# Latent-query attention block: queries of the first token tile alone in the opening, values turned in a bank of their own, ScalarE making the middle part of the keys

## Chip, cores and metric

One NeuronCore of a Trainium2 chip runs the whole program in one launch. The metric is the device time of that launch in microseconds (us). A shorter time is better.

## What is computed

```python
x = x + xattn(layernorm(x), ctx, ctx)      # x (16, 32, 512), ctx (16, 512, 512), 32 heads, 8 kv heads, head 16
x = x + attn(layernorm(x))                 # rotary, causal, 32 tokens, own weights
x = x + x @ w.T + bias                     # w: 512x512 from 3-bit values, one norm per group of 32
...
q = (query @ Wq); k = (key @ Wk); v = (value @ Wv)
scores = jnp.einsum('bhqd,bhkd->bhqk', q, k) * scale
out = jnp.einsum('bhqk,bhkd->bhqd', jax.nn.softmax(scores, axis=-1), v)
...
x_norm = q / 7.0
return (x_norm * (2.0 * n) - n).reshape(-1)
```

The three lines on top are a summary in words; the rest is cut from the reference. All inputs are float32.

## The kernel before

**Engines and order.** The program is written engine by engine (`@block.sync`, `gpsimd`, `scalar`, `vector`, `tensor`); each engine runs its list in order, and semaphores (`wait_ge`, `then_inc`) tie them. Nothing is scheduled by a tool. TensorE is PE in the rows, VectorE is DVE, ScalarE is ACT, GpSimd is POOL, SyncE is SP.

**Tiles.** 512 tokens (16 batches of 32) are four token tiles of 128 rows. The context of a batch is 512 keys by 512 features, loaded already transposed (1 MB). The eight key/value heads are the eight groups g; R = 4 query heads share one.

**Exact products out of bf16.** Keys and queries are split in three bf16 parts: high (a rounded copy), middle (the rounded rest) and low (what is left). For keys: ACT copies bank b_k to `kparts[...,0]` (`key_high`, L576), DVE subtracts to `kres` (`key_residue`, L768), POOL rounds `kres` to the middle part (L468) and subtracts for the low part (L470), both in `key_parts`. Six DMAs of 128 KB from SP (`stack_keys`, L355) copy the parts into six 16-row slots of `kstack`, so that one bf16 matmul adds the six cross products. Queries go through the same four steps (`query_high`, `query_residue`, `query_mid`, `query_low`) into `qparts`, and by six DMAs into `qstack`. The context is split in two f32r parts, `cT_h` (ACT, L611, in the opening L696) and `cT_l` (DVE, L795, in the opening L827), four chunks c each; a projection chunk (`project`, L976 to L978) is three matmuls of 512 columns into b_k or b_v.

**Slots.** After the opening, slot n = 0 to 17 runs a pipeline over batches, with eight steps g: for batch n the scores as rows (L1022, bank b_s or b_x) and their maxima (DVE, L783); for batch n-1 the scores turned, with the maximum taken off by extra rows (L1059, banks b_c), and the exponentials (ACT, L591); for batch n-2 the product with the values (`times_v`, L1001), once per slot behind g = 1. Projection chunks for batches n+1 and n+2 are spread over the steps by the table in `projections`. Values leave b_v through ACT (`vT`, L632, at g = 3), are turned by PE **back into b_v** (L1027, at g = 4), and DVE copies them to `vaug` (`copy_values`, L773, at g = 4); the next V projection (g = 5, chunk 0) writes b_v and waits for that copy (`v_ready`). The middle slots are hardware loops (4 to 11 on PE). In slots 14 and 15 the steps of the second layer are woven in from the table EARLY, the rest follows after slot 17 (LATE).

**SP's order in a slot n:** the context of batch n+3 (waits for the low parts of batch n+1, whose buffer it takes), key parts of batch n+1, query parts of batch n+2.

**The opening.** Context chunks of batch 0, its K and V projection (the last eight matmuls of V begin the fast stretch of PE), layer norm of all four token tiles at once, 16 transposes, then all queries: for each r of four, a sum over four chunks c of f32 matmuls with 512 columns (`first_queries_of`, L1187; each f32 matmul shows as two records), through banks b_c. Then both projections of batch 1, and slot 0. SP sends the first batch's queries as six 32 KB DMAs, then batches 1 to 3 as six of 96 KB (L308). The 3-bit weights are unpacked by DVE between these (`unpack`, L809 to L822) and scaled by POOL in two passes over 128x2048 numbers: times 2n (L555), minus n (L558).

## Time and profile before

| what | value |
|---|---|
| time, median of 3 runs | 336.38 us (335.36 to 337.74) |
| the profiled execution | 338.57 us |
| its span (first to last instruction) | 336.7 us |
| PE busy | 312.5 us, 93% |
| DVE busy | 228.4 us, 68% |
| ACT busy | 186.6 us, 55% |
| POOL busy | 111.0 us, 33% |
| moved by DMA | 41.48 MB, 123 GB/s over the span |

All times in rows are microseconds from the start of the span. A line L768 is line 768 of the kernel before. A busy PE is not PE at its peak: a matmul's record is longer than the distance to the next one, so distances between starts are used.

### The profile page before, as it was taken

The numbers are of one execution on the slowest core, as the hardware profiler recorded it, in microseconds if no ns is written. First come the engines' busy times: TensorE is split into PE (matmuls) and PEld (weight loads), VectorE is DVE, ScalarE is ACT, GpSimd is POOL, SyncE is SP. The second block draws the span as 40 slices with busy tenths as digits, with TensorE's granted clock in tenths as the row PEclk, the third lists the DMA queues.
The fourth block names the chain that finished last, engine by engine and source line by source line (L and its number), as shares of the span: only waits on it lengthen the run. The fifth ranks groups of instructions, "written<-read, shape, count | busy, mean of one in ns | idle before, by whom it ended". The sixth has DMA issues, their size and how long they took to land.

```text
span 336.7 us, 7756 instructions
## 1 busy us (share of the span) xinstructions
PE 312.5 (93%) x2662; PEld 217.2 (64%) x2665; DVE 228.4 (68%) x391; ACT 186.6 (55%) x368; POOL 111.0 (33%) x200
## 2 busy tenths in 40 slices
PE   6699939969999999999999999999999998999996
PEld 2464616647767767767767767766667766766664
DVE  3558778846787777777677687675764369867552
ACT  3344422736876776876776777776766422344220
POOL 1130472422313313313313314224730426662320
PEclk9999967979999999999999999999999999999999
DMA  7991376977769759759879889789500000000002
GB/s 212 412 191 22 135 112 74 202 181 86 180 118 188 180 104 197 185 88 200 184 92 205 182 117 227 181 156 201 146 0 5 2 6 6 9 6 8 2 31 93
DMA packets 39466, 41.48 MB, mean 123 GB/s; under 512 B 19936, under 2 KB 34272, under 8 KB 37216
## 3 DMA queue, kind: packets, MB, share of 16 engines
q1 hardware_dynamic: 39008, 41.00, 59.0%
q8 instruction: 17, 0.28, 0.4%
q10 hardware_dynamic: 432, 0.13, 0.2%
q14 instruction: 9, 0.07, 0.1%
HBM read 24.07 MB, written 1.05 MB: 75 GB/s over the span
## 4 chain that ended last, share of the span: by engine, by line
PE 70%; DVE 12%; DMA 7%; ACT 4%; issue 3%; POOL 2%; SPq 1%; DVEq 0%; ACTq 0%; POOLq 0%
PE b_d L1001 8%; PE b_c L1059 7%; DMA kstack<-kparts 5%; PE b_v L976 4%; PE b_s L1022 4%; PE b_c L1187 4%; PE b_v L977 4%; PE b_v L978 4%; PE b_k L976 3%; PE b_k L978 3%; PE b_k L977 3%; PE b_x L1022 3%; DVE negmax L783 3%; DMA wkv_raw<-in_L_xattn_Wv_dram 2%; DVE vaug L773 2%
## 5 line engine op out<-in xcount | busy, mean ns | idle before, releaser
L591 ACT ACTIVATE region<-b_c 128x512 f32<-128x512 f32 x128 | 74.6, 597 | 46.3 <-PE b_c L1059 26.2
L783 DVE TENSOR_REDUCE negmax<-b_s 128x1 f32<-128x512 f32 x72 | 49.7, 690 | 49.4 <-PE b_s L1022 48.4
L1059 PE MATMUL b_c<-qstack,kstack 108*128 108x128 bf16 x512 | 50.6, 222 | 0.0
L795 DVE TENSOR_TENSOR cT_l<-cx,cT_h 128x512 fp32r<-128x512 f32 x56 | 45.1, 805 | 6.9 <-ACT cT_h L611 6.8
L1059 PEld LDWEIGHTS b_c<-qstack,kstack 108*128 108x128 bf16 x512 | 32.5, 98 | 26.6 <-issue 13.9
L976 PE MATMUL b_k<-cT_h,wkv_h 128*128 128x512 f32 x64 | 36.3, 568 | 7.8 <-DVE cT_l L827 4.2
L477 POOL TENSOR_TENSOR mwide<-negmax,zeros 128x4 bf16<-128x4 f32 x32 | 6.4, 199 | 101.4 <-DVE negmax L783 101.4
L783 DVE TENSOR_REDUCE negmax<-b_x 128x1 f32<-128x512 f32 x56 | 38.2, 681 | 0.9 <-PE b_x L1022 0.8
L976 PE MATMUL b_v<-cT_h,wkv_h 128*128 128x512 f32 x64 | 35.7, 558 | 1.6 <-DVE vaug L773 1.2
L611 ACT ACTIVATE cT_h<-cx 128x512 fp32r<-128x512 f32 x56 | 35.0, 628 | 0.0
L1022 PE MATMUL b_s<-kstack,qstack 96*128 96x512 bf16 x72 | 28.1, 391 | 6.4 <-DMA kstack<-kparts 3.3
L1001 PE MATMUL b_d<-region,vaug 128*17 128x128 f32 x1024 | 31.5, 275 | 0.0
L468 POOL TENSOR_TENSOR kparts<-kres,zeros 128x512 bf16<-128x512 f32 x16 | 18.6, 1161 | 37.8 <-DVE kres L768 37.8
L1001 PEld LDWEIGHTS b_d<-region,vaug 128*17 128x17 f32 x1024 | 26.8, 98 | 2.0 <-issue 0.4
L978 PE MATMUL b_k<-cT_l,wkv_h 128*128 128x512 f32 x64 | 26.7, 418 | 0.2 <-issue 0.2
L977 PE MATMUL b_k<-cT_h,wkv_l 128*128 128x512 f32 x64 | 26.5, 415 | 0.0
L977 PE MATMUL b_v<-cT_h,wkv_l 128*128 128x512 f32 x64 | 26.1, 408 | 0.0
L583 ACT ACTIVATE qstack<-b_d 12x512 bf16<-12x512 bf16 x32 | 18.9, 589 | 13.1 <-PE b_d L988 12.3
L978 PE MATMUL b_v<-cT_l,wkv_h 128*128 128x512 f32 x64 | 26.0, 407 | 0.0
L1022 PE MATMUL b_x<-kstack,qstack 96*128 96x512 bf16 x56 | 22.2, 396 | 0.0
L976 PEld LDWEIGHTS b_k<-cT_h,wkv_h 128*128 128x128 f32 x64 | 13.1, 205 | 10.7 <-DVE cT_l L795 3.8
L470 POOL TENSOR_TENSOR kparts<-kres,kparts 128x512 bf16<-128x512 f32 x16 | 18.9, 1181 | 1.3
(357 smaller groups left out, 584.7 us busy)
## 6 DMA issues: line engine op xcount, KB each, us to landing
cx<-in_ctx_dram SPq DMA_DIRECT2D x15, 1024.0 KB, 5.9
kstack<-kparts SPq DMA_DIRECT2D x96, 128.0 KB, 5.3
qstack<-region SPq DMA_DIRECT2D x76, 32.0 KB, 3.3
cx<-in_ctx_dram SPq DMA_DIRECT2D x4, 256.0 KB, 4.8
xs<-in_x_dram SPq DMA_DIRECT2D x1, 1024.0 KB, 9.4
region<-in_L_xattn_Wq_dram SPq DMA_DIRECT2D x1, 1024.0 KB, 11.6
cx<-in_L_xattn_Wo_dram SPq DMA_DIRECT2D x1, 1024.0 KB, 10.1
cx<-in_L_attn_Wq_dram SPq DMA_DIRECT2D x1, 1024.0 KB, 7.0
```

The costliest lines, as they stand in the source:

```text
L470: nc.gpsimd.tensor_tensor(kparts[:, m % 2, 2], kres[:], kparts[:, m % 2, 1], ALU.subtract).then_inc(k_low, 1)
L583: nc.scalar.activation(qstack[STACK:ROWS, HALF * half:HALF * half + HALF, m % 4], m_rows[STACK:ROWS].unsqueeze(1).to_broadcast([MROWS, HAL ...
L591: nc.scalar.activation(pT[:, g], b_c[g % 2][:].rearrange("p (a n) -> p a n", a=KT), ACT.Exp, scale=SCALE).then_inc(exp_ready, 1)
L611: nc.scalar.activation(cT_h[:, c], cx[:, m % 2, c], ACT.Copy).then_inc(ctx_high, 1)
L783: nc.vector.tensor_reduce(negmax[:, n % 2, g:g + 1], score_bank(n, g, trip)[:], AX, ALU.max, negate=True).then_inc(max_ready, 1)
L795: nc.vector.tensor_tensor(cT_l[:, c], cx[:, m % 2, c], cT_h[:, c].bitcast(F32), ALU.subtract).then_inc(ctx_low, 1)
L976: nc.tensor.matmul(out, wkv_h[:, which, c], cT_h[:, c], start=(c == 0), stop=False)
L977: nc.tensor.matmul(out, wkv_l[:, which, c], cT_h[:, c], start=False, stop=False)
L978: last = nc.tensor.matmul(out, wkv_h[:, which, c], cT_l[:, c], start=False, stop=(c == C - 1))
L1001: last = nc.tensor.matmul(b_d[TILE * j:TILE * j + VW, P * half:P * half + P], vaug[:, m % 4, a, g], pT[:, g, a], start=(a == 0), stop=(a = ...
L1022: nc.tensor.matmul(score_bank(n, g, trip)[:], qstack[0:STACK, g, n % 4], kstack[0:STACK, n % 4, g], start=True, stop=True).then_inc(s_read ...
L1059: last = nc.tensor.matmul(b_c[g % 2][:, P * a:P * a + P], kstack[0:ROWS, m % 4, g, P * a:P * a + P], qstack[0:ROWS, g, m % 4], start=True, ...
```

## The change

1. **Queries by token tile.** `first_queries_of(t, rows)` makes the queries of one token tile t: 16 matmuls of 128 columns each. Tile 0 (batches 0 to 3) is made in the opening; tiles 1 to 3 are made in halves in slot 0, one half in each of the steps g = 0 to 5. Their splits stand on ACT and DVE in slot 0 too. The tokens are loaded as one 256 KB piece (tile 0) and one of 768 KB, with `xwq` between them. The statistics and the row turns are done for tile 0 first. The query DMAs of the opening are six of 128 KB for batches 0 to 3 together.
2. **Unpacking** by DVE moves into slot 0 (g = 0 to 5) and gives 2q/7 - 1, so that POOL scales in one pass, cut in four, in slot 1.
3. **Values** are turned into b_t (up to slot 13) at g = 5, and copied by DVE at g = 6. A V projection waits only until ACT has emptied b_v.
4. **ACT makes the middle part of the keys** (`key_mid`), at g = 3 of the slot, ahead of `vT`. POOL makes only the low part.
5. Moved besides in the opening: `zeros` set first and 11 warming passes for 9, ACT takes all four context chunks ahead of the V weights, key parts of batch 1 move into slot 0 (as do its last projection chunks), the context of batch 2 is loaded behind the key parts of batch 0.

```diff
-                sp.dma_start(xs[:], xf).then_inc(x_loaded, 16)
+                sp.dma_start(xs[:, 0], xf[:, 0]).then_inc(x_loaded, 16)
                 sp.dma_start(xwq, xwq_d.rearrange("(c p) r n -> p c r n", p=P)).then_inc(xwq_loaded, 16)
+                sp.dma_start(xs[:, 1:TILES], xf[:, 1:TILES]).then_inc(xs_loaded, 16)
                 load_ctx(1, 0)
-                sp.wait_ge(ctx_low, C)
-                load_ctx(2, 0)
...
                     stack_keys(0, part)
-
+                sp.wait_ge(ctx_low, C)
+                load_ctx(2, 0)
+                for part, done in ((0, q_high), (2, q_low)):
+                    sp.wait_ge(done, 1)
+                    first_queries_part(sp, part)
                 sp.wait_ge(ctx_low, 2 * C)
                 load_ctx(3, 0)
...
             def key_parts(m, trip):
-                wait(pool, k_res, 1, m, 1, trip)
                 wait_ring(pool, kstack_loaded, m - 2, trip, SLOTS)
-                nc.gpsimd.tensor_tensor(kparts[:, m % 2, 1], kres[:], zeros[:], ALU.add).then_inc(k_mid, 1)
                 wait(pool, k_mid, 1, m, 1, trip)
...
+            def scale_weights(t):
+                some = slice(NGRP // TILES * t, NGRP // TILES * (t + 1))
+                nc.gpsimd.tensor_tensor(wide[:, some], wide[:, some], wnorm[:, some].unsqueeze(2).to_broadcast([P, NGRP // TILES, GS]),
+                                        ALU.mult).then_inc(w_ready, 1)
...
+            def key_mid(m, trip):
+                wait(act, k_res, 1, m, 1, trip)
+                wait_ring(act, kstack_loaded, m - 2, trip, SLOTS)
+                nc.scalar.activation(kparts[:, m % 2, 1], kres[:], ACT.Copy).then_inc(k_mid, 1)
...
+                    if splits_keys(n, g - 2, trip):
+                        key_mid(n + 1, trip)
                     if g == 3 and live(n + 1, trip):
...
+                    if not looped(trip) and n == 0 and g in (2, 4, 6):
+                        query_residue(g // 2)
+                    if not looped(trip) and n == 0 and g in (3, 5, 7):
+                        query_low(g // 2)
+                    if not looped(trip) and n == 0 and g < 6:
+                        unpack(g)
...
-                    if g == 4 and live(n + 1, trip):
-                        copy_values(n + 1, trip)
+                    if g == 6 and live(n + 1, trip):
+                        copy_values(n + 1, value_bank(n, trip), trip)
...
-                    wait(pe, v_ready if which else k_res, 1, m, 0, trip)
+                    wait(pe, vT_ready if which else k_res, 1, m, 0, trip)
...
+            def first_queries_of(t, rows):
+                pe.wait_ge(xhT_ready, t + 1)
+                count(pe, q_res, t - 1)
+                for r in rows:
+                    for c in range(C):
+                        last = nc.tensor.matmul(b_c[t % 2][:, P * r:P * r + P], xwq[:, c, r], xhT[:, c, P * t:P * t + P],
+                                                start=(c == 0), stop=(c == C - 1))
+                if rows.stop == R:
+                    last.then_inc(q_summed, 1)
...
-                    if g == 4 and live(n + 1, trip):
-                        wait(pe, vT_ready, 1, n + 1, 1, trip)
-                        for a in range(KT):
-                            last = nc.tensor.transpose(b_v[:, P * a:P * a + P], vT[:, P * a:P * a + P], ident[:])
-                        last.then_inc(v_transposed, 1)
+                    if g == 5 and live(n + 1, trip):
+                        turn_values(n + 1, value_bank(n, trip), trip)
...
+                    if not looped(trip) and n == 0 and g < 6:
+                        first_queries_of(1 + g // 2, range(R // 2 * (g % 2), R // 2 * (g % 2 + 1)))
```

PE in the opening, before: the rows after the V projection of batch 0. `region` as an input is `xh` under L1204 and `xwq` with `xhT` under L1187.

```order
L1180 MATMUL b_c<-zeros 128x512 x4
L1204 MATMUL b_x<-ident_sb,region 128x128 [waits xh_ready,ident_loaded]
L1204 MATMUL b_s<-ident_sb,region 128x128 [waits xh_ready]
L1204 MATMUL b_c<-ident_sb,region 128x128 [waits xh_ready]
L1208 MATMUL b_v<-ident_sb,vT 128x128 [waits vT_ready]
L1187 MATMUL b_c<-region 128x512 [waits xwq_loaded,xhT_ready]
```

The same place after the change (L1229 turns rows, L1049 makes queries, L1035 turns values).

```order
L1229 MATMUL b_c<-ident_sb,region 128x128 [waits xh_ready,ident_loaded]
L1221 MATMUL b_c<-zeros 128x512 x3
L1049 MATMUL b_c<-region 128x128 [waits xhT_ready,xwq_loaded]
L1049 MATMUL b_c<-region 128x128 x15
L1229 MATMUL b_x<-ident_sb,region 128x128 [waits xh_ready]
L1229 MATMUL b_s<-ident_sb,region 128x128 [waits xh_ready]
L1035 MATMUL b_t<-ident_sb,vT 128x128 [waits vT_ready]
L1001 MATMUL b_k<-cT_h,wkv_h 128x512 [waits k_res,ctx_low]
```

Sixteen matmuls of 512 columns became sixteen of 128 in this place; the other 48 of 128 stand in slot 0, as in this piece of PE's list (its steps g = 2 and g = 5).

```order
L1064 MATMUL b_s<-kstack,qstack 128x512 [waits max_ready]
L1001 MATMUL b_k<-cT_h,wkv_h 128x512 [waits k_res,ctx_low]
L1049 MATMUL b_c<-region 128x128 [waits q_res,xhT_ready]
L1049 MATMUL b_c<-region 128x128 x7
...
L1064 MATMUL b_x<-kstack,qstack 128x512 [waits max_ready]
L1035 MATMUL b_t<-ident_sb,vT 128x128 [waits v_ready,vT_ready]
L1001 MATMUL b_v<-cT_h,wkv_h 128x512 [waits vT_ready,ctx_low]
```

In step g = 5 the turn now stands ahead of the V projection and goes to b_t; in the list before it stands one step earlier and goes to b_v.

ACT in a slot of the loop, before.

```order
L583 ACTIVATE qstack<-b_d 12x4x128 [waits pv_ready]
L626 ACTIVATE o_raw<-b_d 128x256 [waits oraw_transposed,pv_ready]
L591 ACTIVATE region<-b_c 128x512 [waits pv_ready,st_ready]
L276 REGISTER_ALU [waits v_chunk]
L632 ACTIVATE vT<-b_v 128x512 [waits v_transposed]
```

And after.

```order
L597 ACTIVATE qstack<-b_d 12x4x128 [waits pv_ready]
L640 ACTIVATE o_raw<-b_d 128x256 [waits oraw_transposed,pv_ready]
L605 ACTIVATE region<-b_c 128x512 [waits pv_ready,st_ready]
L590 ACTIVATE kparts<-kres 128x512 [waits kstack_loaded1,k_res]
L277 REGISTER_ALU [waits v_chunk]
L648 ACTIVATE vT<-b_v 128x512 [waits v_transposed]
```

The middle part of the keys (L590) stands behind the third exponential of the slot and ahead of the copy of the values.

## Rows read from the trace of the kernel before

**Rows 1.** Windows by stage: length, busy and count by engine, PEclk, DMA share, GB/s.

```profile
23.00:36.50 13.50, 13.48 (x33) 6.07 (x33) 10.85 (x24) 5.71 (x10) 1.35 (x2) 1.00 0.37 108
44.00:57.20 13.20, 9.32 (x29) 5.26 (x30) 11.13 (x13) 0.87 (x3) 5.27 (x6) 0.61 0.82 100
57.20:71.30 14.10, 10.48 (x71) 6.92 (x70) 9.85 (x15) 9.42 (x17) 5.52 (x14) 1.00 0.97 185
...
85.60:227.30 141.70, 139.31 (x1511) 100.70 (x1509) 106.03 (x177) 102.77 (x200) 43.28 (x112) 1.00 0.85 165
```

**Rows 2.** Timeline, opening and slot 0: start, duration, engine, line, operation, idle before.

```profile
11.04 1.27 POOL L547 TENSOR_TENSOR wkv_l<-wkv_raw,wkv_h 128x512 fp32r<-128x512 f32 x1 [9.26 <-ACT wkv_h L712]
...
15.64 0.63 PE L976 MATMUL b_v<-cT_h,wkv_h 128*128 128x512 f32 x1
...
19.39 1.04 PE L1180 MATMUL b_c<-zeros 128*128 128x512 bf16 x4
...
23.02 14.00 PE L1187 MATMUL b_c<-region 128*128 128x512 f32 x32 [0.41 <-ACT region L727]
...
44.02 0.38 PE L1022 MATMUL b_s<-kstack,qstack 96*128 96x512 bf16 x1 [1.52 <-DMA qstack<-region]
...
44.83 3.64 POOL L558 TENSOR_TENSOR region<-region,wnorm 128x2048 f32<-128x2048 f32 x1
45.04 3.98 DVE L795 TENSOR_TENSOR cT_l<-cx,cT_h 128x512 fp32r<-128x512 f32 x1
...
49.08 0.79 PE L976 MATMUL b_k<-cT_h,wkv_h 128*128 128x512 f32 x1 [3.29 <-DVE cT_l L795]
```

**Rows 3.** Timeline, slot 1 and the start of slot 2.

```profile
57.04 0.36 SPq L349 DMA_DIRECT2D cx<-in_ctx_dram  x1
...
71.31 0.39 PE L1022 MATMUL b_s<-kstack,qstack 96*128 96x512 bf16 x1 [3.10 <-DMA kstack<-kparts]
```

**Rows 4.** The page's DMA issues: count, KB each, us from issue to landing.

```profile
xs<-in_x_dram SPq DMA_DIRECT2D x1, 1024.0 KB, 9.4
```

**Rows 5.** Windows, one stretch of the opening; the last two numbers are DMA share and GB/s.

```profile
24.00:26.00 2.00, 2.00 (x6) 0.93 (x5) 1.28 (x4) 0.00 (x0) 1.35 (x2) 1.00 0.45 87
```

**Rows 6.** Timeline of PE, one slot of the loop (136.81 to 149.65).

```profile
136.81 0.38 PE L1022 MATMUL b_s<-kstack,qstack 96*128 96x512 bf16 x1
...
137.27 0.40 PE L977 MATMUL b_k<-cT_h,wkv_l 128*128 128x512 f32 x1
...
143.68 0.38 PE L1022 MATMUL b_s<-kstack,qstack 96*128 96x512 bf16 x1
144.09 0.66 PE L1027 MATMUL b_v<-ident_sb,vT 128*128 128x128 f32 x4
...
145.53 0.38 PE L1022 MATMUL b_x<-kstack,qstack 96*128 96x512 bf16 x1
...
146.37 0.40 PE L977 MATMUL b_v<-cT_h,wkv_l 128*128 128x512 f32 x1
...
149.65 0.38 PE L1022 MATMUL b_s<-kstack,qstack 96*128 96x512 bf16 x1
```

**Rows 7.** Timeline of POOL and ACT in the next slot (from 149.65).

```profile
152.97 1.16 POOL L468 TENSOR_TENSOR kparts<-kres,zeros 128x512 bf16<-128x512 f32 x1 [1.88 <-DVE kres L768]
...
155.36 0.60 ACT L591 ACTIVATE region<-b_c 128x512 f32<-128x512 f32 x1
```

**Rows 8.** Key DMAs (L355): the last two of that slot, then all 96.

```profile
L355 SPq DMA_DIRECT2D kstack<-kparts x2: 594/597/600, 154.8 to 155.4; - x2
DMA to landing us min/median/max: 6.1/6.4/6.6
...
DMA to landing us min/median/max: 3.3/5.3/8.3
```

**Rows 9.** Weight loads of L1187 (group, mean ns); f32 matmuls of 128 columns in the tail.

```profile
L1187 PEld LDWEIGHTS b_c<-region 128*128 128x128 f32 x32 | 6.0, 190 | 7.8 <-issue 7.2 <-ACT region L727 0.6
...
296.56 1.09 PE L1155 MATMUL b_k<-kstack,vaug 128*64 128x128 f32 x16
```

More of the change, by code:

```diff
@@ L289, in splits_keys @@
         def splits_keys(n, g, trip):
-            return g == 1 and (looped(trip) or 1 <= n < B - 1)
+            return g == 1 and (looped(trip) or n < B - 1)
         def wait_queries(eng, m, trip):
@@ L381, in opening @@
                     stack_keys(0, part)
+                sp.wait_ge(ctx_low, C)
[3 more added lines that the diff above has]
+                    first_queries_part(sp, part)
                 sp.wait_ge(ctx_low, 2 * C)
                 load_ctx(3, 0)
-                for part, done in ((0, q_high), (2, q_low)):
-                    sp.wait_ge(done, R)
-                    first_queries_part(sp, part, 0, 1, first_queries)
-                for part in range(3):
-                    first_queries_part(sp, part, 1, 4, next_queries)
             def slot(n, trip):
@@ L414, in slot @@
                         stack_keys(m, part)
+                if not looped(trip) and n == 1:
+                    sp.wait_ge(q_low, TILES)
                 if live(n + 2, trip) and (looped(trip) or n >= 2):
@@ L505, in slot @@
                     max_parts(n, 0, trip)
+                if not looped(trip) and n == 1:
+                    pool.wait_ge(unpacked, 1)
+                    for t in range(TILES):
+                        scale_weights(t)
                 if n == B - 2:
@@ L1003, in times_v, with turn_values @@
                 last.then_inc(pv_ready, 1)
+            def turn_values(m, bank, trip):
+                wait(pe, vT_ready, 1, m, 1, trip)
+                wait(pe, v_ready, 1, m, 0, trip)
+                for a in range(KT):
+                    last = nc.tensor.transpose(bank[:, P * a:P * a + P], vT[:, P * a:P * a + P], ident[:])
+                last.then_inc(v_transposed, 1)
             def projections(n, g, trip):
-                if not looped(trip) and (n, g) in ((0, 0), (0, 1), (0, 3)):
-                    return []
                 ahead, which, c = ((1, 0, 3), (1, 1, 2), (2, 0, 0), (1, 1, 3), (2, 0, 1), (2, 1, 0), (2, 0, 2), (2, 1, 1))[g]
                 return [(n + ahead, which, c)] if live(n + ahead, trip) else []
+            def first_queries_of(t, rows):
+                pe.wait_ge(xhT_ready, t + 1)
+                count(pe, q_res, t - 1)
+                for r in rows:
+                    for c in range(C):
+                        last = nc.tensor.matmul(b_c[t % 2][:, P * r:P * r + P], xwq[:, c, r], xhT[:, c, P * t:P * t + P],
+                                                start=(c == 0), stop=(c == C - 1))
+                if rows.stop == R:
+                    last.then_inc(q_summed, 1)
             def slot(n, trip):
@@ L1198, in opening @@
                     project(0, 1, c, 0)
-                warm(4)
                 pe.wait_ge(ident_loaded, 16)
-                for t in range(TILES):
-                    pe.wait_ge(xh_ready, t + 1)
-                    for c in range(C):
-                        last = nc.tensor.transpose((b_x, b_s, *b_c)[t][:, P * c:P * c + P], xh[:, t, P * c:P * c + P], ident[:])
-                    last.then_inc(xh_transposed, 1)
-                pe.wait_ge(vT_ready, 1)
-                for a in range(KT):
-                    last = nc.tensor.transpose(b_v[:, P * a:P * a + P], vT[:, P * a:P * a + P], ident[:])
-                last.then_inc(v_transposed, 1)
-                for r in range(R):
-                    first_queries_of(r)
-                for which in range(2):
-                    for c in range(C):
-                        project(1, which, c, 0)
+                turn_rows(0)
+                warm(3)
+                pe.wait_ge(xwq_loaded, 16)
+                first_queries_of(0, range(R))
+                turn_rows(1)
+                turn_rows(2)
+                turn_rows(3)
+                turn_values(0, b_t, 0)
+                for which, c in ((0, 0), (0, 1), (0, 2), (1, 0), (1, 1)):
+                    project(1, which, c, 0)
+                pe.wait_ge(xhT_ready, TILES)
             opening()
```

186 lines of the change are left out of this document (90 added, 96 removed).

## The prediction

> **What bounds the kernel now.** I read the windows by stage first, to see where PE, the busiest engine, is not full; then the timeline across each hole; then one slot of the loop, start by start; last the DMAs, since they feed both holes.
>
> The windows [rows 1] show five stages. From 23 to 36.5 PE is full with the first queries. Slot 0 (44.0 to 57.2) has PE at 9.32 of 13.20 us and a granted clock of 0.61. Slot 1 (57.2 to 71.3) has PE at 10.48 of 14.10. Slots 3 to 13 (85.6 to 227.3) are eleven slots of 141.70/11 = 12.88 us with PE at 98%: here PE is the bound, unless its records hide waits. What comes after slot 13 isn't touched by the change.
>
> The timeline [rows 2] says what makes the early holes. The queries of all four tiles take PE from 23.02 for 14.00 us, and slot 0 can't start before their parts have gone through ACT, DVE and a DMA: 44.02, ended by `qstack`. At 45.04 a DVE subtraction of 512 columns lasts 3.98 us, as long as POOL's second scaling pass beside it (44.83, 3.64 us for four times the columns); PE waits 3.29 us for it. A granted clock of 0.61 over the slot says that most of it ran at the lower of the two levels, 1.2 GHz, and this is the slot in which PE stood still. Slot 2 starts at 71.31 after 3.10 us of waiting for `kstack` [rows 3].
>
> In the loop [rows 6], a score and the first pass behind it take 137.27 - 136.81 = 0.46 us when nothing waits. At g = 5 the same pair takes 146.37 - 145.53 = 0.84: 0.38 us of wait for DVE's copy of the values out of b_v. At g = 4 the turn of the values starts 0.41 behind the score instead of 0.23: 0.18 us of wait for ACT's `vT`. So each slot of 149.65 - 136.81 = 12.84 us holds some 0.56 us of waits inside what looks full.
>
> **Opening, up to slot 0.** V's weights bound its projection from below: POOL has their low part at 11.04 + 1.27 = 12.31, but PE began V at 15.64, behind K [rows 2]. ACT now takes the context chunks first, so K is done by about 12.3 and V starts there. V took 19.39 - 15.64 = 3.75 us; at the spacing of 0.23 of the loop [rows 6] it takes 2.8, to 15.1, and with all of it slow 17. The tokens of tile 0 come early enough: all of them land 3.55 + 9.4 = 12.95 [rows 4], 768 KB less at some 400 GB/s is 11.0; statistics, two small activations and 0.5 us of normalising end near 13. Turning tile 0 takes 0.45 (four transposes), ACT's copy 0.6, so its queries start near 16.3. How long they take the trace doesn't show: no f32 matmul has 128 weight columns and 128 moving ones. L1187 shows 14.00/32 = 0.4375 us per record of 512 columns [rows 2], a quarter is 0.11. From below this is the end. From above, the weight load of L1187 (0.19 us [rows 9]) would set the pace if it hid behind nothing. The nearest row is L1155, 64 weight columns against 128: 1.09/16 = 0.068 per record, below its own weight load, so loads do hide. I take 0.12: 32 records, 3.8 us, to 20.1.
>
> The Trainium skill, "TensorE: Matmul & The Clock Gate", sections "LDWEIGHTS (loading the stationary operand)" and "Weight-path perf modes", speaks against this edit: a weight load costs its columns divided by 1.2 in ns whatever the moving side, and the fast load is not for FP32, so cutting 512 columns into 4 times 128 makes four times the loads. L1187's 190 ns per load is no shorter than that rule's 107 ns; L1155 shows such loads hidden. By the rule unhidden this is a rival, below.
>
> Behind the first queries come three tile turns (1.3 us), the value turn (0.45), and nine matmuls of batch 1's projections. Six of those wait: the third context chunk is on ACT behind two row copies, the middle part and two DMA issues, ready near 26.5. PE would arrive at slot 0 at about 28.6 to 30, and its idle of 3 us there may cost clock.
>
> But the DMA comes later. Before, key parts of batch 0, context 2 and the small loads were through at about 25, where the busy share drops to 0.45 [rows 5]. The same bytes stand ahead of the queries now. The six query DMAs are 128 KB each, like a key DMA, and two of those land 160.9 and 162.0, 1.05 apart [rows 8]. 25 + 6 x 1.05 = **31.3** for the start of slot 0, for 44.02. Bounds: 28.6 if the DMAs keep up, 35 if ACT's two DMAs and the small packets add their own time.
>
> **Slots 0 and 1.** PE's work in slot 0: 8 scores x 0.23 = 1.8; 8 projection chunks x 0.70 = 5.6; 48 f32 matmuls, 96 records x 0.12 = 11.5; turns 0.7. Sum 19.6. DVE: before, 11.13 less the 3.3 of stall = 7.8; from the stretch 23 to 36.5, 10.85 less four context subtractions (2.65) = 8.2; some 1.9 more for the rest of the unpacking, one query pair less, a key residue. Sum 17.9, just under PE, and its last context subtraction falls at about 20.5. That one releases SP's load of context 4, and here the end is set by the same chain as before: load issued 57.04, keys landed and slot 2 begun 71.31, 14.3 us [rows 3]. It is a queue of 1 MB, the constants and six key DMAs, and POOL's low part comes only about 1 us later in slot 1, so it hides in that queue. Slot 2 starts at 31.3 + 20.5 + 14.3 = 66.1, for 71.31: **-5.2 us**. So two thirds of the 12.7 us won in the opening go back, because slot 0 now carries 48 matmuls. Bounds: -8 with 28.6, and +3.8 with records of 0.19 (128 x 0.07 = 9 more).
>
> POOL's one pass of 4 x 0.9 us stands in slot 1, behind both key and maximum parts. It can still stretch a DVE subtraction by 0.9; PE waits for keys at the end of that slot in any case, so nothing. If that cover went it would cost up to 1 us. The 3.65 us pass that is dropped and the stall of 3.29 are inside the account of slots 0 and 1.
>
> **Slots 2 to 13, twelve of them.** The two value waits go (up to 0.56 each). What is late next? ACT gains 0.63 us per slot, at 72% before (102.77/141.70 [rows 1]); its exponential behind the new copy is needed a step later, so that hides. The keys don't. POOL began the middle part at 152.97, that is 3.3 us into the slot; ACT can only begin behind the exponential of 155.36 to 155.96, 6.3 into it [rows 7]. Middle part ready at 6.9, low part at 8.1: 2.5 us later than before. SP's last key DMA goes at about 8.25 into the slot. Behind it in SP's list stand the six query DMAs and the next context load, all 2.5 us later too; neither is needed within the slot. Before, the last key DMA was issued 5.75 in and landed 155.4 + 6.6 = 162.0, 12.35 in, just ahead of the next start at 162.5: the queue was full, so a later issue costs less than it is late. With the least landing of 3.3 us for the first middle DMA (issue 6.95, lands 10.3) and 1.05 for each of the two behind, the keys land at 12.4. The slot can't be shorter than about 12.5, while PE alone would allow 12.3. Gain 0.35 per slot, 12 x 0.35 = **-4.2 us**. Bounds: -6.7 (12 x 0.56), and above zero if landings stay at today's.
>
> **Sum.** The profiled execution is 338.57 us (2.2 above the median shown). 338.57 - 5.2 - 4.2 = 329.2; the same 9.4 off the median 336.38 gives **327.0**.
>
> **Rivals.**
> A, the loop wins nothing: with 4.6 us of landing for the low part (8.25 + 4.6 = 12.85) the key wait takes exactly the place of the value waits. For: DMA share 0.85 over the loop. Against: the landings of 6.1 to 6.6 contain the queue. 336.38 - 5.2 = 331.2.
> B, weight loads set the pace: 0.19 per record, slot 2 starts 3.8 later than before; 336.38 + 3.8 - 4.2 = 336.0, no change. For: the 190 ns load. Against: L1155.
> C, slower: the late middle part. If the low part's DMA still takes the row's 6.1 us [rows 8] from its issue at 8.25, it lands at 14.35, and every slot ends there: 12 x 1.5 = 18 - 5.2 = +12.8, 349.2. It decides from a landing of 5.35 on (slot of 13.6, where 12 x 0.75 outweighs 5.2 by 1%); the median of all is 5.3, which speaks for it, but those DMAs stood behind three high parts and 1 MB, and now the queue would have run nearly empty.
> D, the opening wins nothing: slot 0 grows by as much as it starts earlier, because DVE and PE wait for each other on its chain of query splits. Then only the loop: 332.2.
>
> The Trainium skill, "DMA: Bandwidth & Descriptors", section "Issuing engines are not separate DMA queues", says that DMAs from several engines run on the same 16 engines. By that, the two middle query DMAs on ACT's queue win nothing over SP's, as the sum has it; no row here shows the two queues apart.
>
> **How the numbers follow.** Forecast 0.55 (its own range 322 to 331.5), A 0.15, B 0.10, C 0.07, D 0.08, and 0.05 for both gains near their upper bounds (about 321). Low 319.5 takes in the last; high 334 takes in A and D and leaves out B and C, 0.17. A difference of 1% (3.4 us) is about what a measurement of this kernel can tell from no change: faster than 333.0 holds the forecast, most of A and over half of D, 0.77; within 1% most of B and the rests, 0.16; slower C, 0.07.
>
> **What would show it.** Right: the first score at about 31, its wait ended by `qstack`; slot 2 at about 66 after a wait for `kstack`; 32 records of queries in about 3.8 us; slots of 12.5 us in the loop, no wait for `vaug` or `vT` before b_v's matmuls, and small waits for `kstack` at slot starts. Wrong: queries at 6 us (B); slots of 12.85 (A) or over 13.5 (C) with scores waiting for `kstack` each time; slot 0 of more than 25 us with PE waiting for DVE (D).

## The result and the profile after

The changed kernel takes 346.29 us (median of 4 runs, 344.89 to 349.12), the kernel before in the same session 337.06 us (335.36 to 338.42): ratio 1.029, 95% interval 1.020 to 1.037. It is slower by 9 us, where 9.4 us less were forecast. Medians here are over all runs of a kernel, ratios only over those that didn't fall into a slower state of the chip, so the two can differ by about 1%. The profiled execution took 349.12 us with a span of 347.3, 10.6 more than the 336.7 of before. I call slot n the time from the first score of batch n to the first score of batch n+1; the starts come from the timeline of PE.

| | before | after | predicted |
|---|---|---|---|
| slot 0 starts | 44.02 | 35.22 | 31.3 |
| slot 0, slot 1 long | 13.18, 14.11 | 20.94, 15.48 | 20.5, 14.3 |
| slot 2 starts | 71.31 | 71.64 | 66.1 |
| slots 2 to 13 | 155.96 | 164.11 | 151.8 |
| slot 14 long | 14.57 | 16.66 | as before |
| from there to the end | 94.86 | 94.89 | as before |

So 0.3 + 8.15 + 2.1 = 10.6 us, and nearly all of it lies in the loop. Windows by stage, with the columns of [rows 1]: the end of the opening, slot 0, slot 1, slots 3 to 13. Each line has the window and its length, the busy us of PE, of its weight loads, of DVE, ACT and POOL, then the granted clock, the DMA share and GB/s.

```profile
23.00:35.20 12.20, 4.43 (x22) 3.11 (x21) 2.90 (x5) 3.46 (x7) 0.34 (x1) 0.93 1.02 233
35.20:56.20 21.00, 20.98 (x134) 18.93 (x134) 15.66 (x30) 6.43 (x12) 2.36 (x5) 0.88 0.22 41
56.20:71.60 15.40, 10.65 (x71) 6.91 (x70) 11.38 (x18) 10.84 (x20) 9.23 (x17) 0.98 0.86 162
86.90:235.70 148.80, 138.79 (x1507) 103.50 (x1507) 101.39 (x177) 107.48 (x210) 36.29 (x100) 0.98 0.73 158
```

PE did the same work in the loop (138.79 us busy against 139.31) in 148.80 us instead of 141.70. It stood still for 2.4 us of it before and does for 10 us now. The DMA share fell from 0.85 to 0.73, so the queues weren't fuller either. What PE waits for stands in the page's groups; the number behind the bar is busy time, the last part idle time and what ended it.

```profile
L475 POOL TENSOR_TENSOR kparts<-kres,kparts 128x512 bf16<-128x512 f32 x16 | 18.6, 1163 | 121.3 <-ACT kparts L590 121.3
...
L1064 PE MATMUL b_s<-kstack,qstack 96*128 96x512 bf16 x72 | 28.3, 393 | 20.7 <-DMA kstack<-kparts 12.7
```

The same scores before:

```profile
L1022 PE MATMUL b_s<-kstack,qstack 96*128 96x512 bf16 x72 | 28.1, 391 | 6.4 <-DMA kstack<-kparts 3.3
```

The first scores of the slots now wait 12.7 us in all for `kstack`, for 3.3 before, and POOL's low part waits 121.3 us for ACT's middle part. The timeline has the single waits (PE; its idle time is in brackets): after slot 1 as in [rows 3], then at the end of slot 4 and of slot 12.

```profile
35.22 0.58 PE L1064 MATMUL b_s<-kstack,qstack 96*128 96x512 bf16 x1 [4.99 <-DMA qstack<-region]
71.64 0.61 PE L1064 MATMUL b_s<-kstack,qstack 96*128 96x512 bf16 x1 [3.26 <-DMA kstack<-kparts]
113.84 0.39 PE L1064 MATMUL b_s<-kstack,qstack 96*128 96x512 bf16 x1 [2.16 <-DMA kstack<-kparts]
221.53 0.61 PE L1064 MATMUL b_s<-kstack,qstack 96*128 96x512 bf16 x1 [4.81 <-DMA kstack<-kparts]
```

The slots don't share the loss evenly. Slots 8 to 11 take 12.44, 12.38, 12.41 and 12.38 us with no such wait, 0.4 us less than the 12.84 of before. Slots 4 to 7 take 14.67, 14.11, 13.75 and 13.14, and slots 12 and 13 take 17.08 and 14.22. The waits aren't the whole price: three stretches behind waits, in slots 2, 5 and 13, ran at a granted clock of 0.54 to 0.59.

```profile
71.60:78.40 6.80, 6.76 (x71) 4.82 (x74) 2.58 (x4) 1.42 (x3) 0.00 (x0) 0.54 0.52 147
116.00:119.40 3.40, 3.40 (x63) 2.53 (x65) 0.84 (x2) 0.48 (x2) 0.00 (x0) 0.59 1.04 267
221.50:225.20 3.70, 3.67 (x15) 2.51 (x16) 2.16 (x4) 1.11 (x2) 0.00 (x0) 0.58 0.92 304
```

PE is counted busy there, only slower. (The expectations below name slots 4 to 7 also by the starts they end with, 5 to 8.)

The chain of waits across slot 4 names what carries the delay: POOL's low part, its DMA, PE.

```profile
101.16 4.89 issue
106.05 0.03 POOLq L277
106.08 0.00 issue
106.08 1.17 POOL kparts L475
107.26 0.02 issue
107.27 6.45 DMA kstack<-kparts
113.72 0.12 issue
113.84 0.39 PE b_s L1064
```

And SP's list in slot 4 (99.17 to 113.84), where L367 sends queries, L356 loads a context and L362 sends key parts:

```profile
96.27 4.08 SPq L367 DMA_DIRECT2D qstack<-region  x6
100.63 0.36 SPq L356 DMA_DIRECT2D cx<-in_ctx_dram  x1
101.04 6.83 SPq L362 DMA_DIRECT2D kstack<-kparts  x6
108.10 3.93 SPq L367 DMA_DIRECT2D qstack<-region  x6
112.29 1.34 SPq L356 DMA_DIRECT2D cx<-in_ctx_dram  x1
```

The query DMAs run until 100.35, past the start of the slot, because they stand behind late key parts. So the 1 MB context load goes out 1.46 us into the slot, 0.4 ahead of the high key parts. It took 10.2 us to land (5.7 in the slot before). The low part, issued 8.1 us into the slot as worked out, then took 6.45 us to land. In the settled slot from 167.28 the last three key DMAs took 3.5 to 4.2. There too the queries run past the start of the next slot (180.10 for 179.66) and the context load goes out 0.65 us into it, but 1.2 us ahead of the key parts. So an overrun alone doesn't yet make a slot long.

### The profile page after: what moved, and what is told of

Read it like the earlier page. It is cut to its first block, busy times and chain, and to the rows that moved or that the text cites. A ratio compares the mean times of both kernels' runs of the same rounds, so it can differ in the third digit from the quotient of the medians.

```text
span 347.3 us, 7973 instructions
## 1 busy us (share of the span) xinstructions
PE 312.2 (90%) x2759; PEld 229.0 (66%) x2762; DVE 218.5 (63%) x391; ACT 194.5 (56%) x386; POOL 97.0 (28%) x185
## 3 DMA queue, kind: packets, MB, share of 16 engines
HBM read 24.07 MB, written 1.05 MB: 72 GB/s over the span
## 4 chain that ended last, share of the span: by engine, by line
PE 39%; issue 28%; DMA 11%; POOL 8%; DVE 8%; ACT 3%; SPq 2%; POOLq 0%; ACTq 0%; DVEq 0%
PE b_c L1049 4%; PE b_d L1026 3%; DMA kstack<-kparts 3%; DMA qstack<-region 3%; PE b_c L1100 3%; DMA cx<-in_L_attn_Wq_dram 2%; PE b_s L1064 2%; DMA wkv_raw<-in_L_xattn_Wv_dram 2%; DVE negmax L804 2%; POOL mwide L486 2%; POOL kparts L475 1%; PE b_v L1001 1%; PE b_v L1003 1%; PE b_v L1002 1%; PE b_v L1126 1%
## 5 line engine op out<-in xcount | busy, mean ns | idle before, releaser
L475 POOL TENSOR_TENSOR kparts<-kres,kparts 128x512 bf16<-128x512 f32 x16 | 18.6, 1163 | 121.3 <-ACT kparts L590 121.3
L1064 PE MATMUL b_s<-kstack,qstack 96*128 96x512 bf16 x72 | 28.3, 393 | 20.7 <-DMA kstack<-kparts 12.7
L822 DVE TENSOR_TENSOR cT_l<-cx,cT_h 128x512 fp32r<-128x512 f32 x56 | 38.8, 693 | 0.6 <-ACT cT_h L625 0.6
L1001 PE MATMUL b_v<-cT_h,wkv_h 128*128 128x512 f32 x64 | 36.4, 569 | 0.5 <-POOL wkv_l L562 0.5
L1026 PE MATMUL b_d<-region,vaug 128*17 128x128 f32 x1024 | 32.7, 282 | 0.0
L1026 PEld LDWEIGHTS b_d<-region,vaug 128*17 128x17 f32 x1024 | 27.5, 101 | 2.6 <-issue 0.6
L1064 PEld LDWEIGHTS b_s<-kstack,qstack 96*128 96x128 bf16 x72 | 7.0, 97 | 30.3 <-issue 14.7
L1003 PE MATMUL b_k<-cT_l,wkv_h 128*128 128x512 f32 x64 | 25.8, 404 | 0.0
L584 ACT ACTIVATE kparts<-b_k 128x512 bf16<-128x512 f32 x16 | 9.5, 596 | 20.1 <-PE b_k L1003 19.8
```

The lines of the kernel that those rows point to most:

```text
L475: nc.gpsimd.tensor_tensor(kparts[:, m % 2, 2], kres[:], kparts[:, m % 2, 1], ALU.subtract).then_inc(k_low, 1)
L822: nc.vector.tensor_tensor(cT_l[:, c], cx[:, m % 2, c], cT_h[:, c].bitcast(F32), ALU.subtract).then_inc(ctx_low, 1)
L1001: nc.tensor.matmul(out, wkv_h[:, which, c], cT_h[:, c], start=(c == 0), stop=False)
L1003: last = nc.tensor.matmul(out, wkv_h[:, which, c], cT_l[:, c], start=False, stop=(c == C - 1))
L1026: last = nc.tensor.matmul(b_d[TILE * j:TILE * j + VW, P * half:P * half + P], vaug[:, m % 4, a, g], pT[:, g, a], start=(a == 0), stop=(a = ...
L1064: nc.tensor.matmul(score_bank(n, g, trip)[:], qstack[0:STACK, g, n % 4], kstack[0:STACK, n % 4, g], start=True, stop=True).then_inc(s_read ...
```

## Experiments

Theory T says that the late middle part on ACT is the cause; the rivals are named in each expectation. The first four ran together.

**e1**, part 4 undone in the slots.

```diff
+                if looped(trip) or m > 0:
+                    wait(pool, k_res, 1, m, 1, trip)
+                    nc.gpsimd.tensor_tensor(kparts[:, m % 2, 1], kres[:], zeros[:], ALU.add).then_inc(k_mid, 1)
                 wait(pool, k_mid, 1, m, 1, trip)
...
-                    if splits_keys(n, g - 2, trip):
-                        key_mid(n + 1, trip)
```

> The changed kernel with the middle part of the keys made by POOL again in the slots (part 4 undone there, all else kept). Theory T, the copy on ACT stands too late (6.3 us into the slot, POOL's began 3.3 us into it) and holds up SP's list: the 12.7 us of waits for kstack at slot starts between 71 and 230 us and the 2 us of slot 15 go, slots of 12.3 to 12.45, time about 332 to 334. Rival R1, the value turn one step later and its copy by DVE at g = 6 make the context parts and so SP's loads late: waits stay, 344 to 347. Rival R2, the loads of the opening, pushed back, put the transfers of all later slots out of step: waits stay too, 343 to 347, and slots 5 to 8 are the long ones again.

Measured: 330.19 us, ratio 0.983 (0.977 to 0.989). Part 4 alone costs 16 us. The time is below the range of T. Of the waits for `kstack` in the loop two are left, ahead of slots 5 and 13 (1.62 and 1.56 us). Slots 2, 3 and 5 to 11 take 12.08 to 12.71 us, most of them 12.20. Slot 4 is long here too (14.04), but the next one is at 12.17 again: such a disturbance can arise without the late part, and doesn't last then. What starts it I haven't found. R1 and R2 fall.

From the start of slot 2 to that of slot 14, e1 takes 150.80 us and the change 164.11. About 6 of these 13.3 us are longer waits ahead of slots (9.4 for 3.5 in sum). About 6 more lie behind waits: slot 2 takes 15.27 for 12.08, slot 13 takes 14.22 for 12.79, and slot 5, nearly without a wait of its own, 14.11 for 12.17. Those are the three stretches at the lower clock shown above, which e1 hasn't got (its granted clock is 1.00 from 68.30 to 75.10, and behind its waits of 1.62 and 1.56 us as well).

**e2**, the same copy on ACT, one step earlier.

```diff
-                    if splits_keys(n, g - 2, trip):
-                        key_mid(n + 1, trip)
...
+                    if splits_keys(n, g - 1, trip):
+                        key_mid(n + 1, trip)
                     if g == 2 and live(n - 1, trip):
                         exponentials(n - 1, 0, trip)
```

> The changed kernel with ACT's middle part one step earlier, at g = 2 ahead of the first two exponentials, where ACT idles 1.3 us per slot. T: begins about 3.1 us into the slot, the low part is there at 4.9 for 8.1, waits for kstack go; time 331 to 333, slots of 12.3 to 12.45. If the exponentials, 0.6 us later, hold up PE: slots of 12.6 to 13, 335 to 339. R1 and R2: waits for kstack stay, 344 to 347.

Measured: 328.60 us, ratio 0.980 (0.973 to 0.987). This again is below the range of T. Slots 5 to 11 take 12.20 each without a wait. The engine wasn't wrong, the place was: ACT idled just ahead of the exponentials. In its slot from 92.01 (ACT, POOL and SP), the middle part starts 3.3 us into the slot for 6.2, and SP is through with the queries at 101.98, 2.3 us before the next context load at 104.30:

```profile
92.13 0.34 SPq L356 DMA_DIRECT2D cx<-in_ctx_dram  x1
93.88 3.95 SPq L362 DMA_DIRECT2D kstack<-kparts  x6
95.32 0.63 ACT L590 ACTIVATE kparts<-kres 128x512 bf16<-128x512 f32 x1 [0.95 <-DVE kres L789]
96.03 1.16 POOL L475 TENSOR_TENSOR kparts<-kres,kparts 128x512 bf16<-128x512 f32 x1 [1.88 <-ACT kparts L590]
98.05 3.93 SPq L367 DMA_DIRECT2D qstack<-region  x6
104.30 0.34 SPq L356 DMA_DIRECT2D cx<-in_ctx_dram  x1
```

**e3**, part 4 alone on the kernel before (the `key_mid` of the diff at g = 3, POOL's copy left out for batches from 2 on).

> The kernel before with this alone: ACT makes the middle part of the keys at g = 3 in the slots (the opening as it was, values turned in b_v at g = 4). T: waits for kstack come up at slot starts, 343 to 349. R1 and R2: no change, 336 to 338.

Measured: 341.17 us, ratio 1.017 (1.010 to 1.024), between the ranges, nearer to T's; waits for `kstack` do come up (0.84 ahead of slot 7, 2.74 ahead of slot 13), as T said. The same edit costs 4.4 us on slots of 12.84 and 16 us on slots of 12.2. My reading is that it got dear by what part 3 had won; this isn't shown, for the kernel in which it costs 16 has the new opening too, and parts 3 and 4 were not run together on the old one.

**e4**, part 3 alone on the kernel before.

```diff
-                    wait(pe, v_ready if which else k_res, 1, m, 0, trip)
+                    wait(pe, vT_ready if which else k_res, 1, m, 0, trip)
...
-                    if g == 4 and live(n + 1, trip):
+                    if g == 5 and live(n + 1, trip):
                         wait(pe, vT_ready, 1, n + 1, 1, trip)
...
-                            last = nc.tensor.transpose(b_v[:, P * a:P * a + P], vT[:, P * a:P * a + P], ident[:])
+                            last = nc.tensor.transpose(bank[:, P * a:P * a + P], vT[:, P * a:P * a + P], ident[:])
```

> The kernel before with part 3 alone: values turned in b_t at g = 5, copied by DVE at g = 6. By the rows of the loop the two value waits (0.38 and 0.18 us) go: slots of 12.3 if keys allow it, 12 x 0.56 = 6.7 less, 330 to 331; with keys landing 12.35 into the slot as before, slots of 12.4 to 12.7 and 332 to 335. R1: waits for kstack come up, 340 or more.

Measured: 331.61 us, ratio 0.987 (0.983 to 0.990). Slots of 12.20, 0.64 less than before where 0.56 was worked out. e1 is e4 with the new opening: 330.19 against 331.61. The opening and slot 0 together win 1.4 us, less than the scatter of either.

**e5** asks why lateness adds up over slots. A constant `SENT = 3` takes the place of `SLOTS` in `stack_queries` and in the waits for `qstack_loaded`; all else is the changed kernel.

```diff
-                for s in range(SLOTS):
+                for s in range(SENT):
                     sp.dma_start(qstack[HD * s:HD * s + HD, :, m % 4],
```

> The changed kernel with three of the six query DMAs of a slot left out (batches 4 to 15; the three rows they would fill keep older numbers, so part of the scores is not computed from its own queries). The late middle part on ACT stays. Theory S, the late key parts hurt because SP's list (context load 0.6, keys to about 8.7 us, queries 3.9 us behind them) is then as long as a slot of 12.2 to 12.4, so that one late slot pushes the next context load into the next key parts (its landing was 10.2 us at 100.63, for 5.7 at 87.61): SP is 2 us shorter, the chain of late slots ends at once, at most one slot over 13, time 334 to 338. Rival L, it is the keys' own lateness (low part ready 8.1 us into the slot and 4 to 6.5 us of landing behind it) and no list: slots 5 to 8 stay at 13.1 to 14.7 each and the time at 343 to 347.

Measured: 336.09 us (333.67 to 341.24), ratio 0.995 (0.991 to 0.999). The time is in the range of S. Slots 4 to 11 take 12.32 to 12.59, the chain of late slots is gone; slots 2, 12 and 13 stay over 13, where S allowed one. ACT and POOL are as late as ever; only SP's list has room (its slot from 98.43):

```profile
98.16 0.34 SPq L357 DMA_DIRECT2D cx<-in_ctx_dram  x1
100.17 6.94 SPq L363 DMA_DIRECT2D kstack<-kparts  x6
104.62 0.62 ACT L591 ACTIVATE kparts<-kres 128x512 bf16<-128x512 f32 x1
105.32 1.17 POOL L476 TENSOR_TENSOR kparts<-kres,kparts 128x512 bf16<-128x512 f32 x1 [5.64 <-ACT kparts L591]
107.34 2.00 SPq L368 DMA_DIRECT2D qstack<-region  x3
110.63 0.34 SPq L357 DMA_DIRECT2D cx<-in_ctx_dram  x1
```

The middle part starts 6.2 us into the slot here too, but SP is free at 109.34 and the next load goes out at 110.63, ahead of the slot's start (110.87). Three DMAs of 32 KB less are also less traffic; e11 leaves the traffic as it is.

**e11** leaves nothing out and turns SP's order about in the changed kernel.

```diff
                     load_ctx(n + 3, trip)
+                if live(n + 1, trip) and (looped(trip) or n >= 3):
+                    sp.wait_ge(st_ready, passed)
+                    stack_queries(n + 1, trip)
...
-                if live(n + 2, trip) and (looped(trip) or n >= 2):
-                    sp.wait_ge(st_ready, passed)
-                    stack_queries(n + 2, trip)
```

> The changed kernel, nothing left out, with SP's order turned about: the six query DMAs of a batch go one slot later, directly behind the context load instead of ahead of it (and so ahead of the key parts, not behind them). ACT still makes the middle part at g = 3. The bytes and the number of issues are those of the changed kernel. Theory S, the late key parts hurt by pushing the query DMAs and with them the next context load behind the start of the slot: the load goes out within 0.3 us of every slot's start, slots 4 to 7 come to 12.2 to 12.8, 334 to 339 us. Rival N, e5 gained by its three missing DMAs, that is by their packets in the queues: slots 4 to 7 stay at 13 and more, 343 to 347.

Measured: 339.60 us (335.30 to 341.27), ratio 1.002 (0.998 to 1.006): the median lies just above the range of S, the ratio within it. The sign that S named is there only in part. The context load goes out with the start of the slot (112.21 for 112.20) or ahead of it (124.41 for 125.56, where a slot ends in a wait), but slots 3, 4, 5, 7 and 9 still take 14.19, 13.74, 13.36, 13.94 and 13.32, where S had 12.2 to 12.8 for 4 to 7.

**e12** puts the same order on e8 (below), whose middle part is early.

> The kernel of e8 with the same order of SP's list. There the middle part comes early and the list has 2 us to spare, so S expects next to nothing in slots 4 to 11; the query DMAs now compete with the key parts for the queues just before these are waited for: 323 to 327, 2 us more at most.

Measured: 332.35 us (326.72 to 334.88), ratio 0.973 (0.963 to 0.983), against 324.28 and 0.960 for e8. The expectation missed: the order itself costs 4 us by the ratios and 8 by the medians, and six of the slots from 3 to 13 now start with a wait for keys, for one in e8, since the keys stand behind the queries. The same is likely for the long slots of e11. With this order e11 and e12 are 7 us apart by the medians and 10 by the ratios, opening included; with the order of the change the late middle part costs 16. That fits SP's list carrying a part of the loss, but doesn't size it: in the turned order a late part can also hide behind waits that are there without it, and the pairs differ in the opening and in the stretches at the lower clock. A run with the change's order, its bytes and a shorter list on SP (some of the queries issued by another engine) would have parted the two; there is none.

**e6** turns to the opening, which won 8.8 us at slot 0 and nothing at slot 2. On e2, SP's query DMAs go ahead of the load of context 2.

```diff
-                sp.wait_ge(ctx_low, C)
-                load_ctx(2, 0)
                 for part, done in ((0, q_high), (2, q_low)):
                     sp.wait_ge(done, 1)
                     first_queries_part(sp, part)
+                sp.wait_ge(ctx_low, C)
+                load_ctx(2, 0)
```

> The kernel of e2 with one thing turned about in the opening: the four query DMAs of SP go ahead of the 1 MB load of context 2. Theory D, slot 0 waits for query parts that stand behind 1 MB in busy DMA queues (busy share 1.0 to 1.1 from 20 to 32 us; the query DMAs took 5.6 to 8.9 us to land): slot 0 starts at 30.9 to 31.3 (PE is done at 30.8) for 33.17, and slot 2 starts about 2 us earlier, 65.5 to 66.5 for 67.82; time 326 to 327 for 328.6. Rival P, slot 0 has to wait for the context instead, or slot 2's start hangs on something else: slot 0 earlier, slot 2 as before, 328 to 329.

Measured: 328.15 us (323.68 to 329.93). Slot 0 starts at 30.63 for 33.17, with no wait, and slot 2 at 64.24 for 67.82, more than D asked for. The time doesn't follow and lies in the range of P. The profiled spans are 325.0 and 325.4: slots 2 and 3 take 13.70 and 12.81 for 12.09 and 12.10, and slots 7 and 12 another 0.8 and 0.9 more. The windows behind the start of slot 2, first of e2, then of e6, show the reason in the third column from the right, the granted clock.

```profile
67.80:70.00 2.20, 2.18 (x14) 1.49 (x15) 1.66 (x3) 0.98 (x2) 0.00 (x0) 1.00 0.97 410
```

```profile
64.20:66.50 2.30, 2.26 (x10) 1.58 (x11) 1.29 (x2) 0.72 (x2) 0.00 (x0) 0.63 0.70 292
66.50:70.20 3.70, 3.70 (x74) 2.69 (x73) 1.29 (x2) 1.80 (x4) 1.16 (x1) 0.77 0.45 113
```

PE had waited 2.03 us there in e2 and 2.55 in e6, and in e6 it ran partly at 1.2 GHz afterwards.

**e7** fills PE's idle time in the opening with the queries of tile 1.

```diff
-                for which, c in ((0, 0), (0, 1), (0, 2), (1, 0), (1, 1)):
+                for which, c in ((0, 0), (0, 1)):
                     project(1, which, c, 0)
+                first_queries_of(1, range(R))
                 pe.wait_ge(xhT_ready, TILES)
+                for which, c in ((0, 2), (1, 0), (1, 1)):
+                    project(1, which, c, 0)
...
-                    if not looped(trip) and n == 0 and g < 6:
+                    if not looped(trip) and n == 0 and 2 <= g < 6:
```

Tile 3 is turned through bank b_v for this, as b_c is taken.

> e6, and besides the 16 matmuls of token tile 1 (32 records, 3.8 us) taken out of slot 0 and put into the opening where PE stands idle for 3.4 us for the context (23.8 to 27.2). Theory F, slots 0 and 1 are bound by PE's 11.5 us of f32 matmuls put there: slot 0 starts at 31 to 32 and is 16.3 to 17 us long for 20.16, slot 2 starts at 62 to 63.5, time 322.5 to 324.5. Rival V, DVE (14.85 us busy in slot 0) or SP's chain of loads bounds slots 0 and 1: slot 0 over 18.5 us or slot 1 longer by as much, 326 to 328.

Measured: 327.98 us (322.74 to 330.45), ratio 0.977 (0.968 to 0.986). Slot 0 starts at 28.73 and slot 2 at 64.28, as in e6: the 3.8 us taken out of slot 0 came back. The timeline and the windows of PE show how.

```profile
34.07 0.77 PE L1001 MATMUL b_k<-cT_h,wkv_h 128*128 128x512 f32 x1 [3.09 <-DVE kres L789]
34.63 0.63 PE L1002 MATMUL b_k<-cT_h,wkv_l 128*128 128x512 f32 x1
35.06 0.63 PE L1003 MATMUL b_k<-cT_l,wkv_h 128*128 128x512 f32 x1
35.49 3.62 PE L1049 MATMUL b_c<-region 128*128 128x128 f32 x16
```

```profile
28.70:34.07 5.37, 2.25 (x9) 1.31 (x10) 4.16 (x11) 1.74 (x4) 0.00 (x0) 0.93 0.70 275
34.07:38.00 3.93, 3.93 (x15) 3.65 (x16) 2.23 (x5) 1.00 (x2) 1.16 (x1) 0.50 1.05 132
```

By its lengths and its median this is rival V, though slot 0 starts earlier than expected and the profiled run, 322.74 us, is the quickest of the four. With steps 0 and 1 empty PE runs into the key chain, and after the wait of 3.09 us it ran at a granted clock of 0.50.

**e8** puts tile 2 into those two steps.

```diff
-                    if not looped(trip) and n == 0 and 2 <= g < 6:
-                        first_queries_of(1 + g // 2, range(R // 2 * (g % 2), R // 2 * (g % 2 + 1)))
+                    if not looped(trip) and n == 0 and g in (0, 1, 3, 4):
+                        second = (g + (g > 2)) % 2
+                        first_queries_of(2 if g < 2 else 3, range(R // 2 * second, R // 2 * (second + 1)))
```

> e7 with the queries of tile 2 in the steps g = 0 and 1 of slot 0 and those of tile 3 in g = 3 and 4 (there g = 2 to 5). In e7 PE passed g = 0 and 1 without them, then waited 3.09 us for kres at 31.0 and ran at a granted clock of 0.50 from 34.07 to 38. Theory F (PE's f32 work and such a wait bound slot 0): the wait falls under 0.5 us, slot 0 is 15.5 to 16.5 us long for about 18.3, slot 2 starts at 60.5 to 62 for 64.28, time 2 to 3.5 us under e7's profiled 322.7: 319 to 321. Rival V (DVE's chain bounds slot 0): slot 0 stays over 17.5, slot 2 at 63.5 or later, 322 to 325.

Measured: 324.28 us (321.03 to 329.55, 6 runs), ratio 0.960 (0.953 to 0.967). Slot 0 takes 15.73 us with no wait over 0.5, as F said; slot 2 starts at 62.74, a little late of its range, since slot 0 had to wait for `qstack` until 31.39. The time is above the 319 to 321 of F and in the range of V: slots 2 and 13 took 13.70 and 13.68. By its median this is the fastest kernel of the study, 4% under the one before and 22 us under the change; the runs of e7 and e9 overlap with it.

**e9** moves the four constant loads of slot 12 from ahead of that slot's context load to behind its queries.

> e8, and besides the four constant loads of slot 12 moved in SP's list from ahead of the context load to behind the query DMAs of that slot. Theory S (what stands ahead of the context load in SP's list makes the next key parts late): the waits for kstack at the starts of slots 13 and 14 (0.3 to 1.3 us each in e1, e2, e6) go, 1 to 2 us under e8. Rival: these waits come from the 1 MB weight loads or from the volume alone: as e8, within 0.5 us.

Measured: 325.25 us (324.16 to 329.81), as e8. The wait of 0.86 us ahead of slot 13 went, and the 1.43 ahead of slot 14 became 2.92: the loads only made other slots late (13 takes 15.16 and 14 takes 16.28, for 13.68 and 14.66). The expectation failed.

**e10** is e2 again beside e8.

> The kernel of e2 once more, beside e8 and e9 on one chip: 327 to 330.

Measured: 333.03 us (327.57 to 338.32), ratio 0.980 (0.970 to 0.990), as e2 in ratio, above it and above the expectation in time. In its profiled execution slot 0 started at 37.23 after 6.31 us of waiting for `qstack`, where e2 had 33.17 and 2.34. The six query DMAs of the opening went out at the same times in both (21.8 to 24.1) and took 5.6 to 8.9 us to land in e2 and 8.5 to 13.0 here: 4 of the 7 us between the two spans (325.4 and 332.6).

## Why the prediction was wrong

**The value waits: right.** They are gone, and an undisturbed slot takes 12.20 (e1, e2, e4). In the settled slot at 167.28 the turn follows its score by 0.22 us, and no V projection waits, where [rows 6] had 0.41 and 0.84:

```profile
175.29 0.38 PE L1064 MATMUL b_x<-kstack,qstack 96*128 96x512 bf16 x1
175.51 0.60 PE L1035 MATMUL b_t<-ident_sb,vT 128*128 128x128 f32 x4
175.86 0.48 PE L1001 MATMUL b_v<-cT_h,wkv_h 128*128 128x512 f32 x1
```

**The keys in the loop: the step that failed.** "Behind it in SP's list stand the six query DMAs and the next context load, all 2.5 us later too; neither is needed within the slot." The times of ACT and POOL were right to 0.1 us, and so was the settled slot (12.4 for the 12.5 worked out). That one slot was taken for all twelve. The sum of SP's own list was never made: in slot 4 it sent keys until 8.7 us into the slot and queries behind them until 12.9 (112.03), against slots that were to last 12.4. In this trace one late slot pushes the next context load up to the next key parts, those land late again, and so it runs on for four slots; e5, with a shorter list, hasn't got the chain. The four constants and the context of slot 12 show the same list: before, that load went out at 200.75, ahead of its slot (201.00), and now 2.2 us into it. That the late part at this place is the cause is shown by e1 and e2; how much of it goes through the list stays open (e12). The prediction also had no term for the clock behind waits in the loop, which took about 6 us in slots 2, 5 and 13. Its own range for the loop reached "above zero if landings stay at today's", which is what the disturbed slots did. Rival C named the mechanism and its price (a landing of 6.1 us) and was 3 us off the measured time; it was wrong that every slot would end there. It got 0.07 because "the queue would have run nearly empty": the DMA share over the loop did fall to 0.73, but 1 MB stood right ahead of the keys of slot 4.

The Trainium skill, "DMA: Bandwidth & Descriptors", section "Queues, rings and completion order", says that the issuing engine has one ring on each DMA engine and that descriptors are consumed in ring order. By that, 1 MB issued 0.4 us ahead of the key parts is taken up ahead of them on each engine. The trace agrees: from 102.5 to 104.5, after the first two key DMAs had been issued at 101.04 and 102.26, all 93 packets were of 8 KB, the context's size, and none of the keys' 1 KB. The high parts took 6.3 to 6.5 us to land.

**The opening: mis-sized by its start, and partly by chance.** 32 records in 3.8 us was exact (3.81, below); [rows 6] had a nearer row for it than L1155, the four records of L1027 of the same 128 by 128 columns in 144.50 - 144.09 = 0.41 us. And e1 and e2 have 34.5 and 34.7 us from the start of slot 0 to that of slot 2, for 20.5 + 14.3 = 34.8. The start of slot 0 was 33.2 to 37.2 in the six profiles with this opening (after, e1, e2, e5, e10, e11), never 31.3, and 35.22 in the profile after is just past its upper bound of 35. The term that failed is the 25 in "25 + 6 x 1.05". It counts the bytes of context 2 (1 MB) ahead of the queries, but takes their time from a trace in which that load goes out at 13.5; in the change it stands behind the key parts and goes out at 20.91, right ahead of the queries. e6, which takes it out of the way, starts slot 0 at 30.63. With the middle part late, slots 0 and 1 took some 1.3 us more on average (36.4, 36.2 and 35.6 us in after, e5 and e11, for 34.5, 34.7 and 35.3 in e1, e2 and e10). And the 71.31 of the profile before was itself late: the same opening gave slot 2 at 68.6 in e3 and 69.5 in e4. Against their mean of 69.8 the new opening wins 1.5 and 2.0 us in e1 and e2, which start slot 2 at 68.34 and 67.82, and loses 2.7 in e10 (72.51): no gain at slot 2 that stands clear of the scatter. So nearly all of what it saved at slot 0 is given back, where the prediction had two thirds.

**Weight loads: the rival B is out.** The records of L1049 as in [rows 9] (engine, shape, then min/median/max ns), and the opening's 32 on the timeline:

```profile
L1049 PEld LDWEIGHTS b_c<-region x128: 187/192/333, 18.1 to 54.0; 128*128 128x128 f32 x128
```

```profile
18.15 3.81 PE L1049 MATMUL b_c<-region 128*128 128x128 f32 x32
```

A load shows 192 ns and the next record starts 0.12 behind, so the records overlap. By the rule of the Trainium skill, "TensorE: Matmul & The Clock Gate", section "LDWEIGHTS (loading the stationary operand)", 128 columns take 107 ns to load. An estimate from it for the rival, with the load unhidden beside the 0.11 us of a matmul, is over 0.2 us per record; the trace has 0.12, with the loads hidden, and decides.

**What was left out:** the waits ahead of a slot were priced at their own length. At slot 12, SP issues four constants and then the context, this one 2.2 us into the slot, and the high key parts behind them took 7.9 to 8.2 us to land; the change made an old weak place cost 4.81 us.

## What to carry to other kernels

Before an operation is moved to an engine with time to spare, find the place in that engine's list at which it will run, and follow every transfer that waits for it: the same copy cost 16 us at one step and nothing at the step before. Add up each issuing queue's own list per iteration, as for a compute engine; where the sum reaches the period, as here, don't price the transfers by their average landing time alone. Edits made together may not add up: this copy cost 4.4 us on the kernel before and 16 in the change. And put a price on the clock behind every new wait of PE.

## What the runs showed of the hardware

The start of slot 2 gave a row of waits of PE for the same event, with the length of the slot behind it. In five profiles the granted clock stayed at 1.00 behind the wait, and slot 2 took 12.08 (e1, after 1.96 us of waiting), 12.09 (e2, 2.03), 12.11 (e7, 1.87), 12.07 (e10, 2.69) and 12.70 (e3, 1.68, an old slot of 12.84). In the nine others the windows read behind the wait show a granted clock of 0.50 to 0.77, and slot 2 took 13.68 (e9, 1.82), 13.70 (e8, 2.12), 13.70 (e6, 2.55), 13.64 (e12, 2.61), 14.94 (e11, 2.87), 13.92 (e5, 2.92), 14.27 (before, 3.10), 15.27 (after, 3.26) and 13.66 (e4, 3.41). So such a fall cost 1.4 to 3.2 us behind the wait. The length of the wait alone doesn't tell whether it comes: e9 lost the clock after 1.82 us and e10 kept it after 2.69. The windows behind the two waits, first e9, then e10:

```profile
60.40:64.00 3.60, 3.53 (x18) 2.28 (x19) 2.56 (x4) 1.53 (x3) 0.14 (x1) 0.68 0.80 313
```

```profile
72.50:74.50 2.00, 1.99 (x12) 1.40 (x12) 1.47 (x3) 0.80 (x2) 0.00 (x0) 1.00 0.81 332
```

The same 128 KB DMA between on-chip buffers took from 3.3 to 8.9 us to land in the changed kernel, the longest in slot 12, behind the constants and a context load.
